# Softmax maxima of eight heads at a time, and value products in one group, in an attention loop on one core

## The reference

```
q = (query @ Wq.T + bq).reshape(B, Sq, H, Hd).transpose(0, 2, 1, 3)
k = (key @ Wk.T + bk)...;  v = (value @ Wv.T + bv)...
q = q * SCALE
scores = jnp.einsum('bhqd,bhkd->bhqk', q, k)      # 8 x 16 heads, 112 x 375
attn = jax.nn.softmax(scores, axis=-1)
out = jnp.einsum('bhqk,bhkd->bhqd', attn, v)
out = out.transpose(0, 2, 1, 3).reshape(B, Sq, D)
return out @ Wo.T + bo
```

## Time and profile before

| | |
|---|---|
| median of three runs | 595.64 us |
| span of the profiled execution | 594.4 us |
| PE busy | 433.4 us (73%) |
| DVE busy | 424.1 us (71%) |
| ACT busy | 273.5 us (46%) |
| POOL busy | 81.7 us (14%) |

### The profile page before, as it was taken

One profiled execution on the slowest core, in us unless ns is written; L12 is line 12 of the kernel. 1 busy time (PEld: TensorE's weight loads), 2 busy tenths in 40 slices (PEclk: granted clock), 3 DMA queues, 4 the chain that ended last, 5 costly groups with the idle time before them and its releaser, 6 DMA issues.

```text
span 594.4 us, 10573 instructions
## 1 busy us (share of the span) xinstructions
PE 433.4 (73%) x3584; PEld 294.6 (50%) x3584; DVE 424.1 (71%) x1719; ACT 273.5 (46%) x657; POOL 81.7 (14%) x233
## 2 busy tenths in 40 slices
PE   2799699742268899578999999999999664602106
PEld 2468586521146555445677776776455553202103
DVE  7644999899946678978888888864444566275673
ACT  3754544732231644345465556654533553253440
POOL 6791000000032253704000000000000000000000
PEclk9998699855559799999999999999999898855556
DMA  9700003288004977310056958600300272000002
GB/s 278 211 1 2 1 1 117 93 148 169 19 1 132 130 144 160 103 40 0 3 80 97 203 81 147 183 1 2 142 0 2 78 276 72 1 0 1 1 1 62
DMA packets 34666, 47.25 MB, mean 79 GB/s; under 512 B 5541, under 2 KB 32054, under 8 KB 32822
## 3 DMA queue, kind: packets, MB, share of 16 engines
q1 hardware_dynamic: 34614, 46.58, 33.2%
HBM read 37.87 MB, written 8.60 MB: 78 GB/s over the span
## 4 chain that ended last, share of the span: by engine, by line
PE 55%; DVE 25%; ACT 10%; issue 5%; POOL 4%; DVEq 0%; POOLq 0%; ACTq 0%
PE ps L2194 8%; PE ps L2148 4%; DVE PR L1049 4%; PE ps L2135 4%; ACT below L1769 4%; PE ps L2124 4%; PE ps L1916 4%; PE ps L2034 4%; PE ps L1924 3%; PE ps L2110 3%; PE ps L2322 2%; PE ps L1980 2%; DVE prod L1045 2%; DVE below L1395 2%; PE ps L1875 2%
## 5 line engine op out<-in xcount | busy, mean ns | idle before, releaser
L1263 DVE TENSOR_REDUCE negm<-ps 112x1 f32<-112x375 f32 x128 | 65.5, 543 | 9.2 <-PE ps L2124 6.0
L1740 ACT ACTIVATE E<-ps 125x448 f32<-125x448 f32 x96 | 52.0, 543 | 43.0 <-PE ps L2135 42.7
L2295 PE MATMUL ps<-cnt,same 128*128 128x3 bf16 (+4 forms) x40 | 6.9, 172 | 61.6 <-ACT below L1769 41.1
L2124 PE MATMUL ps<-ks,qs 96*112 96x375 bf16 x128 | 42.9, 345 | 1.7 <-DVE negm L1263 0.8
L2148 PE MATMUL ps<-E,v 125*32 125x112 f32 x768 | 42.1, 270 | 0.0
L1251 DVE TENSOR_REDUCE acts<-gel 128x4 f32<-128x448 f32 x32 | 19.8, 621 | 29.3 <-ACT gel L1708 29.1
L2135 PE MATMUL ps<-qs,ks 99*125 99x112 bf16 x384 | 39.2, 224 | 1.2 <-DVE qs L1284 0.7
L2135 PEld LDWEIGHTS ps<-qs,ks 99*125 99x125 bf16 x384 | 33.8, 137 | 9.7 <-issue 6.2
L2295 PEld LDWEIGHTS ps<-cnt,same 128*128 128x128 bf16 (+1 forms) x40 | 4.4, 110 | 65.1 <-issue 65.1
L1708 ACT ACTIVATE gel<-ps 128x448 f32<-128x448 f32 x32 | 17.3, 543 | 29.3 <-PE ps L2194 29.3
L789 POOL CAST kp<-kx 128x750 bf16<-128x750 f32 x8 | 7.1, 884 | 165.7 <-ACT path L1623 125.8
(11 more groups left out here) (388 smaller groups left out, 1117.9 us busy)
## 6 DMA issues: line engine op xcount, KB each, us to landing
ks<-key_parts SPq DMA_DIRECT2D x48, 187.5 KB, 7.0
piw<-fn_process_input_weights SPq DMA_DIRECT2D x8, 1024.0 KB, 4.9
key_parts<-kp SPq DMA_DIRECT2D x48, 93.8 KB
ctx_again<-in_ctx SPq DMA_DIRECT2D x7, 512.0 KB
keys<-kx SPq DMA_DIRECT2D x16, 187.5 KB, 2.1
kx<-keys SPq DMA_DIRECT2D x8, 375.0 KB, 6.8
ctxP<-in_ctx SPq DMA_DIRECT2D x8, 256.0 KB, 6.3
patn<-in_L_ffn_input_patterns SPq DMA_DIRECT2D x1, 2048.0 KB, 15.6
```

The lines of the kernel that those rows point to most:

```text
L1263: drain(dve.tensor_reduce(negm[:, n:n + 1], bank(nm)[0:S, 0:SC], AX.X, ALU.max, negate=True), nm)
L1740: drain(fn(E[:, (KCH * f + c) % 6, :], bank(nm)[0:KC, 0:4 * S], ACT.Exp), nm)
L2124: fill(mm(bank(nm)[0:S, 0:SC], qs[0:SR, u // 4 % 3, n, :], ks[0:SR, u // 4 % 3, n, :], start=True, stop=True), nm)
```

## The change

Three things change. The value products of a unit, which stood in three places of an iteration, are issued together, behind the third score product for the maxima and ahead of the queries. The maxima go in windows of eight heads (two units, w = 0 to 15): GpSimd splits them (four operations on 112x8, ahead of which it waits for DVE's reductions), PE turns them with one product into rows 0 to 23 of bank 7, in every second iteration, ACT copies these rows to `negrow`, and a DMA of SP puts them into rows 96 to 98 of the query stack. DVE's four splitting operations and its copy go. PE waits for that DMA at the first scores of every second unit. Third, `patn` is loaded in four pieces behind the rows of windows 4, 6, 8 and 10, and the loads behind it move with them.

```diff
@@ plan_psum @@
-        if 0 <= f + 1 < 4 * B:
-            p.add(("negT", f + 1), 7)
+        if f % 2 and 0 <= (f + 3) // 2 < 2 * B:
+            p.add(("negT", (f + 3) // 2), 7)
@@ buffers @@
-        negm = rt.take("negm", [S, NH])
-        negp = rt.take("negp", [S, 2, NH, 3], BF16)
+        negm = rt.take("negm", [S, 2, NH])
+        negp = rt.take("negp", [S, 2, 2, 3, NH // 2], BF16)
+        negrow = rt.take("negrow", [3 * NH // 2, 2, S], BF16)
@@ SP @@
-            for b in range(3, B):
-                wait_filled(sp, ("scoreT", 4 * b - 9, KCH - 1))
-                load_stack(b)
...
+            def place_rows(w):
+
+                b, n = w // 2, NH // 2 * (w % 2)
+                wait_drained(sp, ("negT", w))
+                sp.dma_start(qs[SR:SR + 3, b % 3, n:n + NH // 2, :], negrow[:, w % 2, :]).then_inc(rows_placed[w % 2], 16)
+
+            for w in range(2 * B):
+                place_rows(w)
+                b = (w + 3) // 2
+                if w % 2 and 3 <= b < B:
+                    wait_filled(sp, ("scoreT", 4 * b - 9, KCH - 1))
+                    load_stack(b)
+                if w % 2 == 0 and 4 <= w < 12:
+                    m = 4 * (w // 2 - 2)
+                    sp.dma_start(patn[:, m:m + 4, :], pat_in[128 * m:128 * m + 512, :].rearrange("(c p) d -> p c d", p=128)
+                                 ).then_inc(loaded["pat"], 16)
+                if w == 13:
                     sp.dma_start(oiwn[:, :, :], oiw_in.rearrange("(c p) d -> p c d", p=128)).then_inc(loaded["oiw"], 16)
@@ GpSimd, behind the bias @@
+            for w in range(2 * B):
+                b, h = w // 2, w % 2
+                for i in range(3):
+                    wait_drained(pool, ("smax", 4 * b + 2 * h + 1, i + 1))
+                if w >= 4:
+                    wait_filled(pool, ("negT", w - 4))
+                part, rest = negp[:, b % 2, h, :, :], negm[:, b % 2, NH // 2 * h:NH // 2 * h + NH // 2]
+                did(pool.tensor_copy(part[:, 0, :], rest))
+                settle()
+                did(pool.tensor_tensor(rest, rest, part[:, 0, :], ALU.subtract))
+                settle()
+                did(pool.tensor_copy(part[:, 1, :], rest))
+                settle()
+                pool.tensor_tensor(part[:, 2, :], rest, part[:, 1, :], ALU.subtract).then_inc(neg_ready, 1)
@@ DVE @@
-                    if i == 2 and 0 <= f + 1 < 4 * B:
-
-                        nm = ("negT", f + 1)
-                        wait_filled(dve, nm)
-                        n = 4 * ((f + 1) % 4)
-                        drain(dve.tensor_copy(qs[SR:SR + 3, (f + 1) // 4 % 3, n:n + 4, :].rearrange("p n s -> p (n s)"),
-                                              bank(nm)[SR:SR + 3, 0:4 * S]), nm)
...
-                    part = negp[:, u // 4 % 2, :, :]
-                    did(dve.tensor_copy(part[:, :, 0], negm[:, :]))
...
@@ ACT, in iteration f, ahead of the copy of the query stack @@
+                    if c == 2 and f % 2 and 0 <= (f + 3) // 2 < 2 * B:
+                        w = (f + 3) // 2
+                        nm = ("negT", w)
+                        wait_filled(act, nm)
+                        if w >= 2:
+                            act.wait_ge(rows_placed[w % 2], 16 * (w // 2))
+                        drain(fn(negrow[:, w % 2, :], bank(nm)[0:3 * NH // 2, 0:S], ACT.Copy), nm)
@@ PE @@
-                if c == 0:
-                    wait_drained(pe, ("negT", f))
+                if c == 0 and f % 2 == 0:
+                    pe.wait_ge(rows_placed[f // 2 % 2], 16 * (f // 4 + 1))
...
-            def maxima(f):
-
-                nm = ("negT", f)
-                claim(pe, nm)
-                pe.wait_ge(neg_ready, f // 4 + 1)
-                for i in range(4):
-                    ins = mm(bank(nm)[SR:SR + 3, S * i:S * i + S], negp[:, f // 4 % 2, 4 * (f % 4) + i, :],
-                             identb[0:S, 0:S], start=True, stop=True)
-                fill(ins, nm)
+            def maxima(w):
+
+                nm = ("negT", w)
+                claim(pe, nm)
+                pe.wait_ge(neg_ready, w + 1)
+                fill(mm(bank(nm)[0:3 * NH // 2, 0:S], negp[:, w // 2 % 2, w % 2, :, :].rearrange("p e n -> p (e n)"),
+                        identb[0:S, 0:S], start=True, stop=True), nm)
@@ PE, the order within iteration f @@
-                if behind:
-                    value_products(f - 1, 0)
                 if now:
                     scores_less_maximum(f, 1)
                 if ahead:
                     scores_for_maximum(f + LAG, 2)
+                if f % 2 and 0 <= (f + 3) // 2 < 2 * B:
+                    maxima((f + 3) // 2)
+                if behind:
+                    for c in range(KCH):
+                        value_products(f - 1, c)
                 if f + LAG + 1 < 4 * B:
                     queries(f + LAG + 1)
-                if 0 <= f + 1 < 4 * B:
-                    maxima(f + 1)
-                if behind:
-                    value_products(f - 1, 1)
                 if ahead:
                     scores_for_maximum(f + LAG, 3)
                 if now:
                     scores_less_maximum(f, 2)
-                if behind:
-                    value_products(f - 1, 2)
```

More of the change, by code:

```diff
@@ L518, in build_program @@
         stack_loaded = [sem(f"stack_loaded{i}") for i in range(3)]
+        rows_placed = [sem(f"rows_placed{i}") for i in range(2)]
         def counter(eng, s):
@@ L1262, in _ @@
                         n = 4 * (u % 4) + i
-                        drain(dve.tensor_reduce(negm[:, n:n + 1], bank(nm)[0:S, 0:SC], AX.X, ALU.max, negate=True), nm)
+                        if u >= 8 and u % 2 == 0 and i == 0:
+                            dve.wait_ge(neg_ready, u // 2 - 3)
+                        drain(dve.tensor_reduce(negm[:, u // 4 % 2, n:n + 1], bank(nm)[0:S, 0:SC], AX.X, ALU.max,
+                                                negate=True), nm)
                     if i == 1 and b >= 0 and t == 1:
@@ L1305, in _ @@
                         mean_part(2 * (f - 4 * B) + i)
-                if u < 4 * B and u % 4 == 3:
-                    for i in range(3):
-                        wait_drained(dve, ("smax", u, i + 1))
-                    part = negp[:, u // 4 % 2, :, :]
-                    did(dve.tensor_copy(part[:, :, 0], negm[:, :]))
[L1312 to L1318, removed]
             statistics(3, B - 1)
@@ L2251, in _ @@
                 if f == FREE + 1:
-                    pe.wait_ge(loaded["pat"], 16)
+                    pe.wait_ge(loaded["pat"], 64)
                 if FREE + 1 <= f < FREE + 5:
```

## The result

The changed kernel takes 593.09 us (median of 20 runs, 590.53 to 596.92) against 596.35 for the kernel before in as many. The ratio is 0.9946, 95% interval 0.9927 to 0.9965. It is faster by half a per cent, where 1.5 was forecast. The profiled execution has a span of 591.9 us, before 594.4. The median lies in the stated range of 576 to 598, but outside the 580 to 592 that the prediction took as its own.

What follows compares the result with a forecast made beforehand. PE bounds the attention loop: 104.7 to 96.9 us (-7.8), start +0.2, iterations 27 to 31 -2.0, total -9.6; span 584.8, median 586.0, plus 0.5 for small waits gives 586.5 us; range 576 to 598, own range 580 to 592.

Steps and rivals of the forecast that it cites:

- PE's own work: Attention loop: fewer returns and grouped value products cut a plain iteration from 3.46 to 2.74 us if nothing waits.
- Every iteration, bank of the scores: Second L2135 score group waits for the exponential to free its bank: 0.31 us, making an even iteration 3.05.
- costs taken at nothing: DVE's removed work, ACT's extra copy of 24 rows, SP's row and pattern DMAs: all counted as zero.
- Start: Ahead of f=0: DVE operations leave, two maxima products wait for GpSimd; +0.2 us net, bounds -0.5 and +1.
- D: Slower rival: more second-order waits, another 0.3 us per iteration, 596 us, no change; chance 0.15.
- The waits on bank 7 and on pvs: Odd iterations: pvT waits for pvs, the maxima product for bank 7; f%4=1 takes 4.59 us, f%4=3 3.93.
- rival A: GpSimd's chain ends last, PE waits at odd iterations' maxima product; break-even about 2.4 us against 1.00; 603 us, chance 0.09.
- The DMA of the rows: Maxima rows copied at 3.3 in t=1, needed 8.4 us later; about 5 us if queued behind the stack, cover 3.4.
- The clock (E): Rival: PE's clock falls as it idles a fifth of the time, doubling L2135 and L2124; above 620 us, chance 0.03.
- The rule on the shared ports: DVE's tensor_reduce never contends with GpSimd for their shared ports, so the sum stays; otherwise some 6 us of slowing.
- The rule on the tiling mode: Changing tiling mode drains TensorE; a maxima product in another mode than the value products costs the 0.24 bound, +3 us.
- rival C: Most waits hidden: bank waits of 0.31 per iteration, 0.63 and 0.2 in t=1 and 3 absent; 574 us, chance 0.17.

Runs made afterwards that it cites:

- queries first: Changed kernel with the queries of unit f+6 issued ahead of the value products, behind the maxima product: ratio to the kernel before 0.9927.
- without the loads: Key-stack loads for batches 3 to 7 left out: of the changed kernel, ratio 0.9937, batch 15.56; with queries also ahead of value products, 0.9867, batch 15.04.
- both moves: Changed kernel with PE's order queries, value products, then maxima product: ratio to the kernel before 0.9887.
- maxima product late: Changed kernel with the maxima product behind the 24 value instructions instead of ahead of them: ratio to the kernel before 0.9883.
- the kernel with halves: Changed kernel with four edits of PE's and ACT's order, patterns' loads behind window 12, key stack loaded in halves of eight heads: 575.05 us, ratio 0.9626.

## Why the prediction was wrong

The direction was right, the size was not: 9.6 us forecast in the profiled execution, 2.5 seen; 9.1 and 3.3 in the medians.

**PE's own work: right.** 24 value instructions in 0.71, one return instead of three, and a plain iteration of 3.20 that is 2.79 without its wait of 0.41 (forecast 2.74). With the queries first the bank's wait comes in its place, and the plain iteration is 3.09 (forecast 3.05).

**The step that failed is "Every iteration, bank of the scores".** I took that bank as the only thing that the new order leaves open from one iteration to the next, at 0.31 us. The query stack's copy is the other, and it ends later: the first product of the next iteration reads it. I had the copy in my schedule as something that ACT does, and put under "costs taken at nothing" only ACT's idle time. The wait of 0.41 takes the place of the 0.31, and, since it stands ahead of oT and wo instead of behind them, these no longer hide it: 0.15 + 0.35 + 0.41 a batch. Moving the queries takes 0.52 of this 0.94 back (batch 15.04 without the loads). The other 0.42 is mostly of the new order: in each of the two odd iterations PE takes 2.01 us from the maxima product to the next iteration's first product (329.43 to 331.44), where the sum had 1.78, as the last L2141 now stands behind value products and pays a return, and the step from the maxima product to the queries is 0.14, not the 0.05 of the sum. No run takes these apart. Over the 23 iterations from f = 4 to 26 the 0.94 is 5.4 us.

**Start: mis-sized.** It stands in the sum as "+0.2 net" ahead of f = 0. The first maxima product waits 0.8 us and the second 0.9 for GpSimd's chain, the queries stand behind them, and the next iteration's first product waits for these. From the first queries to those of f = 3 the changed kernel takes 26.3 us where the old one took 24.9, and by the sum it would have been some 1.4 less; in the kernel with both moves it is 23.4. This 2.8 and the 5.4 are more than the 6.1 us by which the loop missed its forecast; the rest, 2 us the other way, lies in the last iterations (15.7 forecast for 27 to 31, 15.1 measured) and those with ln3. That it makes up for a part of the miss is luck. Of the rivals D is the nearest in kind: another 0.3 us an iteration, where the batch's 0.94 is 0.23. The remaining microsecond of the miss in the span is in code that the change leaves alone.

**The waits on bank 7 and on pvs: right**, in place and size: f%4 = 1 4.59 and 4.62. **GpSimd: right.** Its chain of four is 1.0 us, and rival A's margins of 1.15 and 0.49 stand beside 1.03 and 0.85 in the trace (from the chain's end to the maxima product); a chain of 2.1 us made the kernel slower than before by 0.9%, where the break-even had been put at 2.4, with a larger gain to lose. **The DMA of the rows: right**, PE never stood ahead of L2152 without a releaser. **The clock (E)** did not fall in the loop of the changed kernel. It did where PE stood for 2.6 us, and once or more in three other variants (maxima product late, both moves, GpSimd's copy five times).

**The rule on the shared ports** (the Trainium skill, "SBUF — State Buffer", Who interferes with whom): the trace agrees, the longest of the 128 reductions took 550 ns with GpSimd at work beside 31 of them and 550 before. **The rule on the tiling mode** (the Trainium skill, "TensorEngine Tiling (Array Packing)", Key Properties): in the trace of the changed kernel the value products begin 0.10 us behind the maxima product (338.89 and 338.99), but PE had waited ahead of it, so one side is not seen. In the kernel with halves the maxima product (L2191 there) stands between the value products and the next score product without a wait, and costs 0.03 in the chain that ended last:

```profile
322.18 0.03 PE ps L2191
```

A return is paid there with or without it, and no further drain was seen; the bound of 0.24 was not reached, the 0.05 was about right for that place. With the queries behind it, it is 0.14 (329.43 to 329.57 in the run without loads).

**What no rival had:** the key stack. Its loads need 10.5 to 11.3 us from first issue to last landing, and the kernel before came for it 0.3 to 1.3 us later than that. With the 4.1 us from that product to the next loads (328.13 to 332.24), the floor of a batch is 14.7 to 15.4, an estimate from these rows. The forecast's own batch of 14.62 was already at its lower edge, and rival C, at 574 with most waits gone, could not have come without other loads. The prediction had "6.6 us to landing", which is one load's; six are issued 0.44 apart and share the queue, and it never added them up. The changed kernel does not touch this floor, as the run without loads shows. The kernels with moves in PE's order do: there part of the gain was given back.

## What to carry to other kernels

When work is taken from between a producer and its reader on the critical engine, list every reader across the loop's edge, and not only the one that now waits by the bank plan: here the copy of the stack was hidden by exactly the instructions that were grouped elsewhere. Before shortening a loop, work out the floor that its transfers set (first issue to last landing, plus what stands between use and next issue); a transfer that is just in time, here by 0.2 us, shows no wait and becomes the bound at once. When grouping saves an engine time, put the producer of the next iteration's input ahead of the group, and what waits for another engine behind it: with that, ACT's two copies moved forward and earlier loads, the same change gives 3.7% instead of 0.5%.

## What the runs showed of the hardware

A wait for a DMA appears on PE as "issue", with no releaser: the gaps ahead of a batch's first product ended 0.09 us behind the last landing (327.71 and 327.80; 326.53 and 326.62), and were gone without the loads. It can also stand under another engine's name, as at 327.35 in the kernel with the maxima product late. A gap of 2.6 us in a loop that was busy otherwise was followed by a granted clock of 0.71 and then 0.58 (324 to 327 and 327 to 329 us), so partly and then mostly the lower level, 1.2 GHz. f%4 = 3 took 7.8 us, and 3.6 once the gap was gone: a late transfer cost 4.2 us a batch where the gap itself was 2.6. The length of one gap does not tell whether the clock falls: it stayed at 1.00 behind 1.23 us (queries first) and 1.43 us (both moves), and fell behind 0.58 and 1.08 us shortly after each other (maxima product late). Loads of 93.8 KB landed in 3.1 us in the median, and six of them in about 6 from first issue to last landing, where loads of 187.5 KB took 6.5 and 10.5 to 11.3.
